# First pass of a graph kernel: who issues the full-width loads, and in what size

## The reference

```
h  = relu(layernorm(x))
z  = leaky_relu(lap_mul(adj, h) @ W1 + b1)      # lap_mul(A, x) = d * (A @ (d * x)), d = 1/sqrt(row sums of A)
S  = exp(-dist(z_i, z_j) / 2), kept for the 4 nearest j of each row i only
x  = x + lap_mul(S + adj, h) @ W2 + b2
h  = relu(layernorm(x))
x  = x + h @ W_self.T + (adj @ h) @ W_neigh.T + b
```

## Time and profile before

| what | value |
|---|---|
| median of 3 runs | 1475.83 us (1465.95 to 1481.83) |
| the profiled execution | 1477.74 us, of which span 1475.9 us |
| mean granted TensorE clock | 0.873 |
| busy: PE / DVE / ACT / POOL | 72% / 59% / 28% / 52% |
| HBM read, written | 251.07 MB, 39.85 MB |
| first pass, part A | about 4 to 336 us |
| first pass, part B | about 336 to 491 us |

### The profile page before, as it was taken

How to read it: one execution, slowest core, us unless ns; L and a number is a source line. 1 busy time by engine, 2 the same in 40 slices (tenths; PEclk the granted TensorE clock), 3 DMA queues, 4 the chain that set the end, 5 groups by cost and what they waited for, 6 DMA issues and landing times.

```text
span 1475.9 us, 12647 instructions
## 1 busy us (share of the span) xinstructions
PE 1063.8 (72%) x3170; PEld 606.6 (41%) x3170; DVE 870.8 (59%) x888; ACT 406.8 (28%) x997; POOL 773.0 (52%) x1076
## 2 busy tenths in 40 slices
PE   0327277787979885999991878888776637778588
PEld 0113133333434564777771334443332314445355
DVE  3335363565856465999996657575665525545453
ACT  1425346560301252555551000000000011212121
POOL 9999989796432032444443265545343013535454
PEclk9957678798989897999996999889898868989889
DMA  9999999999999587344348999999998399999892
GB/s 197 250 207 230 199 240 189 221 220 209 206 197 215 124 171 184 131 153 164 131 153 167 229 240 238 220 247 214 216 234 200 83 204 219 228 221 227 208 254 68
DMA packets 227462, 291.67 MB, mean 198 GB/s; under 512 B 35936, under 2 KB 192864, under 8 KB 227424
## 3 DMA queue, kind: packets, MB, share of 16 engines
q0 software_dynamic: 56320, 110.41, 33.9%
q1 hardware_dynamic: 98528, 113.72, 30.2%
q10 hardware_dynamic: 72576, 67.12, 20.2%
HBM read 251.07 MB, written 39.85 MB: 197 GB/s over the span
## 4 chain that ended last, share of the span: by engine, by line
DMA 27%; PE 22%; POOL 16%; DVE 13%; issue 8%; ACTq 8%; ACT 3%; SPq 2%; DVEq 0%; POOLq 0%
DMA araw<-in_adj_dram 23%; POOL araw L366 12%; DVE tr L851 5%; ACTq L359 5%; PE ps L1262 3%; PE ps L1263 3%; PE ps L1264 3%; PE ps L1265 3%; DMA t_st<-keys_scratch,block_row 3%; PE ps L1169 3%; PE ps L1318 2%; PE ps L1280 2%; ACTq L781 2%; POOL sq_rows L602 2%; DVE out_t L1059 2%
## 5 line engine op out<-in xcount | busy, mean ns | idle before, releaser
L851 DVE STREAM_TRANSPOSE tr<-araw 128x2048 f32<-128x2048 f32 (+3 forms) x244 | 441.2, 1838 | 314.3 <-DMA araw<-in_adj_dram 213.4
L1280 PE MATMUL ps<-tr,ys 128*128 128x512 f32 x512 | 257.1, 659 | 92.9 <-DVE tr L851 51.2
L366 POOL DMA_DIRECT2D araw<-in_adj_dram x512 | 302.1, 599 | 17.3 <-DVE tr L851 10.4
L1169 PE MATMUL ps<-tr,ys 128*128 128x512 f32 x448 | 236.3, 678 | 49.3 <-DVE tr L851 49.1
L602 POOL TENSOR_TENSOR sq_rows<-tr,zt_lo 128x2048 fp32r<-128x2048 f32 x28 | 126.8, 4538 | 161.9 <-ACT zt_lo L787 161.9
L1280 PEld LDWEIGHTS ps<-tr,ys 128*128 128x128 f32 x512 | 105.7, 213 | 230.2 <-issue 177.6
L712 ACT ACTIVATE araw<-ps,nsq 128x1024 f32<-128x1024 f32 x128 | 142.9, 1117 | 135.7 <-PE ps L1265 109.4
L1169 PEld LDWEIGHTS ps<-tr,ys 128*128 128x128 f32 x448 | 92.9, 216 | 167.6 <-issue 106.6
L561 POOL DMA_INDIRECT zt_lo<-neighbour_table,idx_st x128 | 130.3, 1018 | 46.0 <-issue 41.1
L1262 PE MATMUL ps<-sq_rows,pick 128*128 128x512 f32 x256 | 104.2, 407 | 33.6 <-POOL zs_lo L478 19.5
L634 ACT ACTIVATE ps<-araw 128x256 f32<-128x256 f32 x304 | 111.4, 366 | 34.0 <-DMA araw<-in_adj_dram 28.9
(11 more groups left out here) (139 smaller groups left out, 1112.9 us busy)
## 6 DMA issues: line engine op xcount, KB each, us to landing
araw<-in_adj_dram SPq DMA_DIRECT2D x136, 512.0 KB
araw<-in_adj_dram POOLq DMA_DIRECT2D x528, 128.0 KB, 9.8
araw<-in_adj_dram ACTq DMA_DIRECT2D x120, 512.0 KB
keys_scratch<-araw SPq DMA_DIRECT2D x64, 512.0 KB, 3.6
araw<-in_adj_dram POOLq DMA_DIRECT2D x32, 256.0 KB, 11.3
araw<-in_adj_dram POOLq DMA_DIRECT2D x16, 448.0 KB, 16.5
araw<-in_adj_dram POOLq DMA_DIRECT2D x16, 384.0 KB, 17.7
araw<-in_adj_dram POOLq DMA_DIRECT2D x16, 320.0 KB, 11.6
```

Of the source, the lines that this page charges most:

```text
L366: gp.dma_start(araw[R * q + first:R * q + R:SPREAD, slot], adj_v[q, first:R:SPREAD, g, :, c0:c0 + CHUNK_COLS]).then_inc(a_first_in[slot], DMA)
L851: return v.transpose(out.rearrange("p t (m s) -> p t m s", s=R), src)
L1169: pe.matmul(acc[bank], ys[:, c * GROUPS + first + i], ring1[:, (k + i) % RING1], start=start and i == 0, stop=stop and i == tiles - 1).the ...
L1280: ins = pe.matmul(acc[bank], src[:, j * U + i], tr[:, j % TSLOTS, i], start=j == 0 and i == 0, stop=j == GROUPS - 1 and i == U - 1)
```

## The change

In part A of the first pass POOL keeps quarters 0 and 2, still in transfers of 8 partitions: 8 transfers of 128 KiB for a chunk. Quarters 1 and 3 are issued by SP, each as one transfer of 32 partitions and 512 KiB: 2 for a chunk, 64 in all. SP does this right after its first bias, before its wait on `z_mm`, and makes the same waits for a free slot as POOL does. The quarters from SP report to `a_in`, so each consumer of a chunk waits on two semaphores, and the later passes count from an offset (`WHOLE_A`). Part B and the later passes issue the same transfers as before.

```diff
+SPREAD_QUARTERS = (0, 2)
+WHOLE_QUARTERS = (1, 3)
...
-            loads_in[n % SLOTS] += (SPREAD if n < len(part_a) else chunks) * QD * DMA
+            loads_in[n % SLOTS] += SPREAD * len(SPREAD_QUARTERS) * DMA if n < len(part_a) else chunks * QD * DMA
...
+        SPREAD_IN = SPREAD * len(SPREAD_QUARTERS) * DMA
+        WHOLE_IN = len(WHOLE_QUARTERS) * DMA
+        WHOLE_A = GROUPS * WHOLE_IN
...
         def load_spread(gp, slot, g, c0):
 
-            for quarter_pair in ((0, 2), (1, 3)):
-                for first in range(SPREAD):
-                    for q in quarter_pair:
-                        gp.dma_start(araw[R * q + first:R * q + R:SPREAD, slot],
-                                     adj_v[q, first:R:SPREAD, g, :, c0:c0 + CHUNK_COLS]).then_inc(a_first_in[slot], DMA)
+            for first in range(SPREAD):
+                for q in SPREAD_QUARTERS:
+                    gp.dma_start(araw[R * q + first:R * q + R:SPREAD, slot],
+                                 adj_v[q, first:R:SPREAD, g, :, c0:c0 + CHUNK_COLS]).then_inc(a_first_in[slot], DMA)
+
+        def slot_free(eng, n):
+
+            if n >= SLOTS:
+                was = consumed[n - SLOTS]
+                if was[0]:
+                    eng.wait_ge(t_ready, was[0])
+                if n - SLOTS < LOADS_A:
+                    eng.wait_ge(diag_ready, was[1])
+                    if act_sums(part_a[n - SLOTS][0], part_a[n - SLOTS][1]):
+                        eng.wait_ge(part_act, was[3])
+                    else:
+                        eng.wait_ge(part_dve, was[2])
+
+        def load_first(gp):
 
             for n in range(LOADS1):
+                slot_free(gp, n)
                 if n < LOADS_A:
                     g, c, _ = part_a[n]
+                    load_spread(gp, n % SLOTS, g, c * CHUNK_COLS)
...
+        def load_first_whole(sp):
+
+            for n, (g, c, _) in enumerate(part_a):
+                slot_free(sp, n)
+                load(sp, n % SLOTS, g, c * CHUNK_COLS, CHUNK_COLS, WHOLE_QUARTERS)
...
             sp.dma_start(bias[:], b1.partition_broadcast(P)).then_inc(bias_in, DMA)
+            load_first_whole(sp)
             sp.wait_ge(z_mm, GROUPS)
...
-                act.wait_ge(a_first_in[c], (g + 1) * PER_LOAD * SPREAD)
+                act.wait_ge(a_first_in[c], (g + 1) * SPREAD_IN)
+                act.wait_ge(a_in[c], (g + 1) * WHOLE_IN)
...
-                v.wait_ge(a_first_in[c], (g + 1) * PER_LOAD * SPREAD)
+                v.wait_ge(a_first_in[c], (g + 1) * SPREAD_IN)
+                v.wait_ge(a_in[c], (g + 1) * WHOLE_IN)
...
-                    v.wait_ge(a_in[c], (g + base_group + 1) * PER_LOAD)
+                    v.wait_ge(a_in[c], (g + base_group + 1) * PER_LOAD + WHOLE_A)
```

More of the change, by code:

```diff
@@ L361, in load_spread @@
         def load_spread(gp, slot, g, c0):
-            for quarter_pair in ((0, 2), (1, 3)):
-                for first in range(SPREAD):
-                    for q in quarter_pair:
-                        gp.dma_start(araw[R * q + first:R * q + R:SPREAD, slot],
-                                     adj_v[q, first:R:SPREAD, g, :, c0:c0 + CHUNK_COLS]).then_inc(a_first_in[slot], DMA)
-        def load_first(eng, quarters):
-            for n in range(LOADS1):
[L372 to L381, removed]
+            for first in range(SPREAD):
[14 more added lines that the diff above has]
+        def load_first(gp):
+            for n in range(LOADS1):
+                slot_free(gp, n)
                 if n < LOADS_A:
                     g, c, _ = part_a[n]
-                    load_spread(eng, n % SLOTS, g, c * CHUNK_COLS)
+                    load_spread(gp, n % SLOTS, g, c * CHUNK_COLS)
                 else:
@@ L387, in load_first @@
                     for i, c in enumerate(chunks):
-                        load(eng, n % SLOTS, g, (c * GROUPS + GROUPS - tiles) * R, tiles * R, quarters, i * tiles * R, a_first_in)
+                        load(gp, n % SLOTS, g, (c * GROUPS + GROUPS - tiles) * R, tiles * R, (0, 2, 1, 3), i * tiles * R, a_first_in)
+        def load_first_whole(sp):
+            for n, (g, c, _) in enumerate(part_a):
+                slot_free(sp, n)
+                load(sp, n % SLOTS, g, c * CHUNK_COLS, CHUNK_COLS, WHOLE_QUARTERS)
         def load_chunk(eng, g2, g, c, quarters):
@@ L502, in keep_top @@
                 gp.tensor_copy(idx[:, bass.ds(it, 1), :].rearrange("p o k -> p (o k)"), i8[:, par, 0:TOPK]).then_inc(top_kept, 1)
-            load_first(gp, (0, 2, 1, 3))
+            load_first(gp)
             gp.wait_ge(zl_done, GROUPS)
```

## The result

The changed kernel took **1513.3 us** at the median, the kernel before 1470.9 us beside it: the ratio is **1.032, with a 95% interval of 1.024 to 1.040**. The profiled execution took 1510.62 us, with a span of 1508.8. The forecast was 1467 us in a range of 1440 to 1497. It was wrong in sign and outside its range.

A forecast was written before the change was run, and what follows sets the result against it. Part A was taken as paced by arrival of `adj`, with DMA full and POOL's issue nearly tied. 5 + 4 = 9 us off 1477.74 gave 1469, and the median, 1.9 us lower, 1467 us; range 1440 to 1497.

The forecast's parts named there:

- POOL's freed 151 us: Part A: POOL drops 256 of 512 issues, 151 us of its time; worth only what DMA can then do more.
- the second waits: ACT and DVE in part A: one more semaphore instruction ahead of each chunk, while both wait for DMA anyway; priced 0.
- SP's issues: Part A: SP gains 64 issues at 2.1 us each, 134 us, with nothing else to do then; priced 0.
- The middle stretches: Part A at 222 and 223 GB/s, where POOL's issue may set the pace; 222 again was forecast.
- the pace of the same four sums: DVE's last-chunk sums in part A: 9.5 us a chunk forecast, 8.6 for the faster rival, 10 and over for the slower.
- the slower rival: Part A: SP's quarters trail POOL's half and SP's queue then works alone; 10.7 us a chunk, about 1504 us; chance 0.22.
- My sign in DVE's waits: DVE's waits for `adj` in part A stay above 120 us; for the faster rival they fall by 25.
- the faster rival: Part A: POOL's issue held the middle stretches, two queues fill DMA better; 25 to 35 us less, about 1446; chance 0.36.
- the rate term: Part A: POOL's and SP's mixture at 220 GB/s, 9.5 us a chunk against 9.69; 5 us less over 28 chunks.
- The bound on the low side: Low end of the rate in part A: 175 GB/s, what one queue did nearly alone, up to 10.7 us a chunk.
- The few us behind part A: Behind part A: POOL, free earlier, issues its narrow loads while SP's quarters still arrive; 3 to 4 us back.

The follow-up runs named there:

- the run with opposite halves: The changed kernel with POOL on quarters 0 and 1 and SP on 2 and 3, so the queues write different partition halves: 1.000, median 1480.7 us.
- the runs with fewer issues on POOL: The changed kernel with only one quarter on SP and three on POOL, in three assignments: 0.994, 0.988 and 0.989 of the kernel before.

## Why the prediction was wrong

**Right.** That part A is paced by arrival and DMA is full; that POOL's freed 151 us buy nothing by themselves; that the second waits and SP's issues cost nothing (the run with opposite halves has both, at 1.000, though an issue of SP took 4.3 us at the median there and 5.2 in the changed kernel, not the 2.1 that I took). The middle stretches moved with the rate of DMA and not with POOL's load. The landmark that I named for it, the pace of the same four sums, showed it at once: 10.51 us, the slower rival's "10 and over". My sign in DVE's waits did not: up to 385 us only 94.1 us are put down to `adj`, less than the 120.4 of before, as for the faster rival. But each chunk now has two waits, and these rows are new (0 to 385 us):

```profile
DVE part L892 <- issue: 60.3, 8, 10.3
...
DVE tr L867 <- issue: 21.3, 7, 5.8
```

That they are waits for the same loads is likely and not shown.

**The step that failed** is the rate term: "I take 2.097 MB / 220 GB/s = 9.5 us a chunk for the mixture". The runs showed 189 GB/s, and 10.51 us: the 24 chunks between the two sums cost 19.6 us more, where I had 5 less for 28 of them, and what lies ahead of them 20.8 us more (the last sum of group 1 came at 124.23, not 103.41 us). The rows it came from were sound. The inference was not: I took two equal rates (POOL alone, SP with ACT) to be a property of the bytes and gave it to the mixture too: "A third scheme of issue gives the same rate". But in the stretch of the earlier trace rows SP has quarters 0 and 1 and ACT has 2 and 3, which is the assignment that the run with opposite halves restored at no loss. The change chose POOL 0 and 2, SP 1 and 3. The bound on the low side, 175 GB/s, was in the text; its value was used only for a queue that works alone. A rate term of 0, the other value that I had considered, would have missed as well.

**The few us behind part A** did not show: DVE waited 5.79 us there instead of 3.42. Why is not shown.

**The slower rival** had the sign, and 1504 us is near 1513. Its mechanism is not what costs the time: with opposite halves SP's quarters trail too and POOL waits 155 us for slots, at no cost, and POOL alone loses as much with no second queue at all (1.031). That the time came near is luck. What may be right in it is that an unbalanced stream is slow: clear on one queue, within the noise of the timings with two, and the smaller part.

**The faster rival** did not come about. Its first half, POOL's issue at 9.4 us a chunk, came into reach only once better pairs had raised DMA to 231 GB/s, and even there the runs with fewer issues on POOL were no faster.

The Trainium skill, "SBUF — State Buffer", section "Door 1: The DMA port swizzle", has partitions 0 to 63 on one half of the DMA ports. The runs bear on it: with one queue 29 to 35 us more in part A for pairs on one half, 51 with the same columns; with two queues 10 to 15, which the timings don't separate. That section says nothing of which columns are read together, and by the profiles that was two thirds of this loss or more (27 to 32 us of some 40).

**What stays open** is why the columns matter. A quarter of a row of `adj` is 1,024 float32 columns, so quarters 0 and 2 lie 8 KiB apart, and so do 1 and 3; 0 and 1, 2 and 3, 1 and 2 are 4 KiB apart, 0 and 3 are 12. With half of the loads on SP, the two assignments with even quarters on one queue and odd ones on the other were at 1.025 and 1.032, the three others at 1.000, 1.002 and 1.004. On POOL alone and with both halves written, pairs of an even and an odd quarter were at 0.981 and 0.988 and pairs of one parity at 1 (the kernel before). With 0 and 2 as a pair and 1 and 3 as whole quarters, so one half at a time for those, it was 1.031. This is a pattern of the addresses in HBM and no mechanism; no run changed the row length or the distance of the quarters, which would test it.

## What to carry to other kernels

When DMA engines are full, the rate is still not a constant of the kernel: ask which addresses are in flight together on both ends, and take a rate only from a stretch with the same assignment. A change of queue that also changes who carries which part is two changes; cross them before believing either. Where pieces of one matrix row are loaded in pairs, try the pairings (here three, one line each): the best was 1 to 2% better than the one in use, as much as the best split between queues and with a smaller edit.

## What the runs showed of the hardware that I had not expected

- Between 40 and 300 us DMA shares of 0.98 to 1.05 went with 189, 193, 201, 218 and 231 GB/s for the same 1 KiB pieces. So a share near 1 doesn't tell that bytes flow at the best rate. POOL's queue alone reached 102.4% with pairs on one half, so a share over 1 doesn't need two queues.
- Transfers of 8 partitions on SP's queue: 84% busy engines and 14% more time for the kernel, while POOL's queue carries them at 1.000 and those of 16 partitions at 1.008.
- Which quarters of the columns were read together: 27 to 32 us of part A with two queues, 17 to 23 with one. The mechanism stays open.
